# Expert outputs scattered with addition onto the residual in DRAM

## The reference

```python
h = x' + attention(layernorm(x'))                 # x' is layer 1's normalised input
z = layernorm(h); probs = softmax(z @ router)     # 4096 x 8
top_p, top_i = top_k(probs, 2); top_p /= sum(top_p)
# the rows of each expert, in order, up to cap = 1280; what is beyond is dropped
exp_in = the rows z of expert e, padded with zero rows      # 8 x 1280 x 128
exp_out = gelu(exp_in @ moe_w1[e]) @ moe_w2[e]              # 128 -> 512 -> 128
moe = zeros.at[token].add(exp_out * top_p)        # each token: at most two addends
return h + moe                                    # added to x with the other part
```

## Time and profile before

| | us |
|---|---|
| median of 3 runs | 1261.8 (1260.59 to 1263.59) |
| the profiled execution, as timed | 1267.76 |
| its span, first to last instruction | 1266.0 |
| PE busy | 986.8 (78%) |
| DVE busy | 737.2 (58%) |
| ACT busy | 625.4 (49%) |
| POOL busy | 572.5 (45%) |

### The profile page before, as it was taken

One profiled execution on the slowest core, in us unless ns is written; L12 is line 12 of the kernel. 1 busy time (PEld: TensorE's weight loads), 2 busy tenths in 40 slices (PEclk: granted clock), 3 DMA queues, 4 the chain that ended last, 5 costly groups with the idle time before them and its releaser, 6 DMA issues.

```text
span 1266.0 us, 21239 instructions
## 1 busy us (share of the span) xinstructions
PE 986.8 (78%) x6531; PEld 626.0 (49%) x6564; DVE 737.2 (58%) x1565; ACT 625.4 (49%) x1155; POOL 572.5 (45%) x633
## 2 busy tenths in 40 slices
PE   7699999873999898898989858466567785799960
PEld 4355544572444444454445335344345453699950
DVE  6677760122666566656666454897864556644435
ACT  6555554301776576666766636233256454234410
POOL 3200000268474554646632203987422757865650
PEclk9899999996999899999999979677688878799985
DMA  4011102351101011001010089000010101122216
GB/s 124 34 67 66 66 39 66 100 194 26 26 18 26 14 23 24 20 18 26 18 26 18 1 118 207 1 1 1 1 33 16 49 27 58 46 86 94 79 47 178
DMA packets 67228, 65.89 MB, mean 52 GB/s; under 512 B 6562, under 2 KB 60268, under 8 KB 65104
## 3 DMA queue, kind: packets, MB, share of 16 engines
q1 hardware_dynamic: 52560, 53.46, 15.8%
q0 software_dynamic: 4608, 6.61, 1.6%
q10 hardware_dynamic: 9984, 4.80, 1.4%
HBM read 29.90 MB, written 29.43 MB: 47 GB/s over the span
## 4 chain that ended last, share of the span: by engine, by line
PE 37%; DVE 21%; ACT 6%; issue 5%; DMA 2%; POOL 2%; DVEq 0%; SPq 0%; ACTq 0%; POOLq 0%
DVE B_mneg L1058 6%; PE banks L2069 5%; PE banks L1866 5%; PE banks L2061 4%; PE banks L1838 4%; PE banks L1887 3%; PE banks L1852 3%; PE banks L1991 3%; ACT B_qt L1511 2%; DVE D_dmx L1161 2%; DVE D_pr L1171 2%; PE banks L1944 1%; DVE D_gun L1203 1%; DMA F_back<-y_dram 1%; PE banks L1840 1%
## 5 line engine op out<-in xcount | busy, mean ns | idle before, releaser
L1058 DVE TENSOR_REDUCE B_mneg<-banks 128x2 f32<-128x256 f32 (+3 forms) x256 | 208.3, 823 | 144.6 <-PE banks L1840 138.3
L1520 ACT ACTIVATE B_pt<-banks 128x1024 f32<-128x1024 f32 (+3 forms) x256 | 177.4, 707 | 96.8 <-PE banks L1852 92.8
L724 POOL TENSOR_SCALAR_AFFINE_SELECT B_pt<-B_pt 128x512 f32<-128x512 f32 x128 | 81.4, 636 | 201.3 <-ACT B_pt L1520 195.2
L1838 PE MATMUL banks<-B_kp,B_qt 128*128 128x128 bf16 (+1 forms) x511 | 128.9, 307 | 2.1 <-DVE B_mneg L1058 0.7
L1852 PE MATMUL banks<-B_qt,B_kp 128*128 128x256 bf16 (+3 forms) x480 | 106.4, 299 | 19.0 <-DVE B_mneg L1058 14.6
L1840 PE MATMUL banks<-B_mask_q,B_identb 128*128 128x128 bf16 x512 | 103.9, 223 | 0.1
L1590 ACT ACTIVATE D_pr<-banks,D_dmx 128x512 f32<-128x512 f32 x64 | 44.0, 687 | 120.7 <-DVE D_dmx L1161 120.6
L900 POOL DMA_INDIRECT y_dram<-F_yo,F_ide x80 | 81.1, 1013 | 48.8 <-DVE F_yo L1367 24.6
L1866 PE MATMUL banks<-B_pt,B_vp 128*32 128x512 f32 (+3 forms) x1024 | 97.4, 453 | 6.0 <-issue 5.3
L858 POOL DMA_INDIRECT rows_dram<-F_xs,F_rowi x64 | 63.7, 995 | 77.2 <-DVE F_xs L1239 44.6
L694 POOL CAST B_identb<-ident 128x128 bf16<-128x128 f32 x1 | 0.3, 291 | 202.4 <-ACT C_eo L1493 202.4
(11 more groups left out here) (269 smaller groups left out, 2239.0 us busy)
## 6 DMA issues: line engine op xcount, KB each, us to landing
comb_dram<-C_comb SPq DMA_DIRECT2D x8, 1024.0 KB, 3.8
C_cst<-comb_dram SPq DMA_DIRECT2D x8, 1024.0 KB, 4.8
B_kp<-B_kt SPq DMA_DIRECT2D x64, 128.0 KB, 2.4
rows_dram<-D_zeros SPq DMA_DIRECT2D x8, 645.0 KB, 18.4
F_xe<-rows_dram SPq DMA_DIRECT2D x8, 645.0 KB, 4.0
C_w<-w_in SPq DMA_DIRECT2D x16, 256.0 KB, 2.8
y_dram<-D_zeros SPq DMA_DIRECT2D x2, 2048.0 KB, 18.4
F_gw<-mw_in SPq DMA_DIRECT2D x16, 256.0 KB, 3.0
```

The lines of the kernel that those rows point to most:

```text
L724: g.affine_select(out=w, in_=w, compare_op=ALU.is_ge, fill=0.0, base=0, pattern=[[0, G], [1, P]], channel_multiplier=-1).then_inc(B_md, 1)
L1058: v.tensor_reduce(mneg[:, g % 2, qt, 2 * hp:2 * hp + 2], banks2[pair_of_banks(item)][:, :, 0:(qt + 1) * P], X, ALU.max, negate=True).then_ ...
L1520: a.activation(pt[:, 2 * hp:2 * hp + 2, PT_AT[kt]:PT_AT[kt] + w], banks2[pair_of_banks(item)][:, :, 0:w], ACT.Exp).then_inc(B_ex, 1)
L1838: t_.matmul(dst, qt1[:, g % 2, hp, qt * P:(qt + 1) * P], kp[:, g % NG, hp, h, 0:(qt + 1) * P], start=True, stop=False)
```

## The change

A row carries its token's share as a 130th value, and its row number now names the token's row in one array `acc_dram`, 2048 spare rows and then the 4096 tokens. Empty places carry the number of a spare row of their own, so they are written too (zeros, onto the first 1280 rows, which are cleared). `y_dram` and its clearing are gone. SP stores x, with both attention parts in it, into `acc_dram` once GpSimd's sums are done, and GpSimd waits for that before it begins with the experts. VectorE multiplies the outputs by the share as it takes them out of PSUM, for which it waits until GpSimd has copied the shares. The scatters add onto `acc_dram`. Since the same token can come from two experts, GpSimd waits after each expert until its ten scatters have landed. At the end two DMAs, on SP's and on ACT's queue, copy `acc_dram` to the output, 1 MB each. The shares are worked out four times, for 1024 tokens each, within `choose`, `place_rows` and ScalarE's list.

```diff
-RW = D + 1
+RW = D + 2
 CAP = 1280
+SPARE = 2048
...
         yield t0 + 11.0, ("r", h, 0)
-    yield 216.0, ("d", 0, 0)
+        yield t0 + 10.9, ("d", h, 0)
...
@@ sync
             for e in range(EXP):
                 sp.dma_start(rows_dram[e * CAP:(e + 1) * CAP, :].rearrange("(p n) d -> p n d", p=P),
-                             zeros[:].unsqueeze(1).broadcast_to([P, CAP // P, RW])).then_inc(D_z, 16)
-
-            for k in range(2):
-                sp.dma_start(y_dram[k * B * T:(k + 1) * B * T, :].rearrange("(p n) d -> p n d", p=P),
-                             zeros[:, 0:D].unsqueeze(1).broadcast_to([P, TILES, D])).then_inc(D_z, 16)
+                             zeros[:]).then_inc(D_z, 16)
+            sp.dma_start(acc_dram[0:CAP, :].rearrange("(p n) d -> p n d", p=P),
+                         zeros[:, :, 0:D]).then_inc(D_z, 16)
...
             for par in range(2):
                 load_rows(0, par)
             sp.sem_inc(G_zf, 2)
+            sp.wait_ge(F_xo, 1)
+            for b in range(B):
+                sp.dma_start(acc_dram[SPARE + b * T:SPARE + (b + 1) * T, :].rearrange("(i p) d -> p i d", p=P),
+                             x[:, b * NT:(b + 1) * NT, :]).then_inc(G_acc, 16)
...
-            with sp.Fori(0, B) as b:
-                sp.wait_ge(G_xr, b + 1)
-                sp.dma_start(out[bass.ds(b * T, T), :].rearrange("(i p) d -> p i d", p=P),
-                             x[:, bass.ds(b * NT, NT), :]).then_inc(s_out, 16)
-            sp.wait_ge(s_out, 16 * B)
+            half = B * T // 2
+            sp.wait_ge(G_zs[0], 16 * CT * (EXP // 2))
+            sp.wait_ge(G_zs[1], 16 * CT * (EXP // 2))
+            sp.dma_start(out[0:half, :].rearrange("(p n) d -> p (n d)", p=P),
+                         acc_dram[SPARE:SPARE + half, :].rearrange("(p n) d -> p (n d)", p=P)).then_inc(s_out, 16)
+            sp.wait_ge(s_out, 16 * 2)
...
@@ gpsimd
+            pool.wait_ge(G_acc, 16 * B)
             with pool.Fori(0, EXP // 2) as pr:
                 for par in range(2):
                     pool.wait_ge(G_x[par], pr * 16 + 16)
                     pool.wait_ge(G_zf, at(pr, par, 1, 1))
                     pool.sem_inc(turns, 1)
+                    g.tensor_copy(she[:, par, :], xe[:, par, :, D + 1])
                     g.tensor_copy(ide[:, par, :], xe[:, par, :, D].bitcast(I32)).then_inc(G_id, 1)
...
-                                out=y_dram[:, :], out_offset=bass.IndirectOffsetOnAxis(ap=ide[:, par, m:m + 1], axis=0),
-                                in_=yo[:, par, m, :], in_offset=None, bounds_check=2 * B * T - 1, oob_is_err=False
-                            ).then_inc(G_zs[par], 16)
+                                out=acc_dram[:, :], out_offset=bass.IndirectOffsetOnAxis(ap=ide[:, par, m:m + 1], axis=0),
+                                in_=yo[:, par, m, :], in_offset=None, bounds_check=SPARE + B * T - 1, oob_is_err=True,
+                                compute_op=ALU.add).then_inc(G_zs[par], 16)
+                    pool.wait_ge(G_zs[par], pr * (16 * CT) + 16 * CT)
+                    pool.sem_inc(turns, 1)
...
@@ vector, choose and place_rows
                 dve.sem_inc(F_mk, 1)
+                v.tensor_tensor(e2[:, tiles], top2[:, tiles], top1[:, tiles], ALU.subtract).then_inc(F_d, 1)
...
                     own.link(v.tensor_reduce(row[:, k, tiles], one_hot[:, h], X, ALU.add))
+                shares = [xs[:, 2 * hq:2 * hq + 2, k, :, D + 1] for k in range(2)]
+                dve.wait_ge(F_e, hq + 1)
+                own.link(v.tensor_scalar(e2p[:, tiles], e2[:, tiles], 1.0, None, ALU.add))
+                own.link(v.reciprocal(shares[0], e2p[:, tiles].rearrange("p (q t) -> p q t", t=NT)))
+                v.tensor_tensor(shares[1], e2[:, tiles].rearrange("p (q t) -> p q t", t=NT), shares[0], ALU.mult)
                 for k in range(2):
...
@@ vector, the experts
                             dve.wait_ge(G_zf, it * 2 + (e + 1))
-                        v.tensor_copy(yo[:, e, n0:n0 + n, :], bank[4 + (3 * e + c) % 2][:, 0:n * D].rearrange(
-                            "p (n d) -> p n d", d=D)).then_inc(G_ys, 1)
+                            dve.wait_ge(G_id, it * 2 + (e + 1))
+                        v.tensor_tensor(yo[:, e, n0:n0 + n, :], bank[4 + (3 * e + c) % 2][:, 0:n * D].rearrange(
+                            "p (n d) -> p n d", d=D), she[:, e, n0:n0 + n].unsqueeze(2).broadcast_to([P, n, D]),
+                            ALU.mult).then_inc(G_ys, 1)
...
@@ scalar, behind the experts
-            for par in range(2):
-                act.wait_ge(G_zs[par], 16 * CT * (EXP // 2))
-            act.sem_inc(G_bu, 2)
-            with act.Fori(0, B // 2) as hb:
-                for par in range(2):
-
-                    act.wait_ge(G_bu, at(hb, par, 1, 1))
-                    for k in range(2):
-                        act.dma_start(back[:, par, k, :, :], y_dram[bass.ds(hb * (2 * T) + (par * T + k * B * T), T), :]
-                                      .rearrange("(t p) d -> p t d", p=P)).then_inc(G_bk[par], 16)
+            half = B * T // 2
+            act.wait_ge(G_zs[0], 16 * CT * (EXP // 2))
+            act.wait_ge(G_zs[1], 16 * CT * (EXP // 2))
+            act.dma_start(out[half:2 * half, :].rearrange("(p n) d -> p (n d)", p=P),
+                          acc_dram[SPARE + half:SPARE + 2 * half, :].rearrange("(p n) d -> p (n d)", p=P)
+                          ).then_inc(s_out, 16)
```

More of the change, by code:

```diff
@@ L453, in build @@
         drs, oms = Dm("drs", [P, TILES]), Dm("oms", [P, TILES])
-        zeros, junk = Dm("zeros", [P, RW]), Dm("junk", [P, 2, NT, D])
+        zeros, junk = Dm("zeros", [P, CAP // P, RW]), Dm("junk", [P, 2, NT, D])
         nmr = Dm("nmr", [P, TILES])
         desc, first_row = Dm("desc", [P, EXP]), Dm("first_row", [P, EXP])
-        ids = Dm("ids", [P, 2, TILES], I32)
+        ids = Dm("ids", [P, TILES], I32)
         tri, ones = Dm("tri", [P, P]), Dm("ones", [P, P])
         top1, top2 = Dm("top1", [P, TILES]), Dm("top2", [P, TILES])
-        share, e2 = Dm("share", [P, 2, TILES]), Dm("e2", [P, TILES])
+        e2, e2p = Dm("e2", [P, TILES]), Dm("e2p", [P, TILES])
         row = Dm("row", [P, 2, TILES])
-        kept = Dm("kept", [P, 2, TILES])
         memD1 = ctx.enter_context(ExitStack())
@@ L528, in build @@
         G_zs = [sem("G_y_scattered_even"), sem("G_y_scattered_odd")]
-        back = Fm("back", [P, 2, 2, NT, D])
-        G_bk, G_bu = [sem("G_back_even"), sem("G_back_odd")], sem("G_back_used")
-        G_xr = sem("G_x_ready")
+        G_acc = sem("G_sums_begun")
         memF.close()
@@ L796, in _ @@
             own.link(g.memset(zeros[:], 0.0))
-            g.iota(zeros[:, D:RW].bitcast(I32), pattern=[[0, 1]], base=2 * B * T, channel_multiplier=0).then_inc(D_z, 1)
+            g.iota(zeros[:, :, D].bitcast(I32), pattern=[[1, CAP // P]], base=0, channel_multiplier=CAP // P).then_inc(D_z, 1)
             own.link(g.memset(sc[:], NEG))
@@ L854, in scatter_rows @@
                 if q == 0:
-                    pool.wait_ge(D_z, 16 * (EXP + 2) + 1)
+                    pool.wait_ge(D_z, 16 * (EXP + 1) + 1)
                 for t in range(NT):
@@ L1235, in deviations @@
                                        op1=ALU.mult).then_inc(F_r, 1)
-                dve.wait_ge(F_const, 5)
+                dve.wait_ge(F_const, 4)
             def row_ids(q):
-                v.tensor_copy(xs[:, q, :, :, D].bitcast(I32), ids[:, :, q * NT:(q + 1) * NT]).then_inc(F_id, 1)
+                v.tensor_copy(xs[:, q, :, :, D].bitcast(I32), ids[:, q * NT:(q + 1) * NT].unsqueeze(1)
+                              .broadcast_to([P, 2, NT])).then_inc(F_id, 1)
             def wide(small):
@@ L1285, in place_rows @@
                 ins.then_inc(F_row, 1)
-            def shares():
-                v.tensor_tensor(e2[:], top2[:], top1[:], ALU.subtract).then_inc(F_d, 1)
-                own.link(v.tensor_scalar(kept[:], row[:], float(EXP * CAP), None, ALU.is_lt))
-                dve.wait_ge(F_e, 1)
-                own.link(v.tensor_scalar(share[:, 0], e2[:], 1.0, None, ALU.add))
-                own.link(v.reciprocal(share[:, 0], share[:, 0]))
-                own.link(v.tensor_tensor(share[:, 1], e2[:], share[:, 0], ALU.mult))
-                own.link(v.tensor_tensor(share[:], share[:], kept[:], ALU.mult))
             for kind, a_, n in D_PLAN.order:
@@ L1326, in _ @@
                     place_rows(a_)
-                elif kind == "d":
-                    shares()
             dve.wait_ge(D_rms, 1)
@@ L1375, in _ @@
             own.end_loop(EXP // 2)
-            dve.wait_ge(F_xo, 1)
-            with dve.Fori(0, B // 2) as hb:
-                own.loop(hb, 2 * 2)
-                for par in range(2):
-                    dve.wait_ge(G_bk[par], hb * 32 + 32)
-                    for k in range(2):
-                        for t in range(NT):
-                            i = hb * (2 * NT) + (par * NT + t)
-                            xi = x[:, bass.ds(i, 1), :].squeeze(1)
```

(11 more changed lines are left out.)

7 lines of the change are left out of this document (3 added, 4 removed).

## The result

The changed kernel takes 1298.85 us (median of 4 runs, 1298.53 to 1299.29), the kernel before on the same chip 1262.69 us (4 runs, 1260.59 to 1264.27): ratio 1.0288, interval 1.0270 to 1.0305. So it is slower by 36 us, where 1254.0 was forecast, and it lies above the end of the range, 1286. The profiled execution of after took 1299.29 us as timed, its span is 1297.5 us; before has 1266.0. The medians lie further apart (36 us) than the spans (31.5 us), since the profiled execution of the kernel before was 5 us longer than its median (1267.76 and 1262.69).

The account below looks back on a forecast made before the run. TensorE was taken to bound the experts at 16.92 us each, GpSimd close behind. Last landing 1240.5 + 8v plus a 9.7 us tail gave 1258.2 us span with v = 1.0, median 1254.0; range 1244 to 1286 us.

Parts of the forecast that it names:

- v: Extra cost of ten adding scatters over ten plain ones, up to their landing: taken as 1.0 us, ends 0 and 6.9.
- term 1: Clearing at 739 us: the larger zero tile costs nothing, covered by GpSimd's idle time; 1.1 us without that cover.
- term 2: Shares worked out with the rows: 0.7 us more on the chain from the last row numbers to GpSimd's sums.
- term 3: Start of the experts: GpSimd waits 9.0 us for the stored x, bounds 6.9 and 16.6 us.
- R: Time when expert 0's row numbers and shares are copied and ready: 1108.1 us.
- term 4: Experts' loop: GpSimd's round closes on itself through landing, copies and eviction, 16.62 us plus v, against TensorE's 16.92 us.
- term 5: End of the kernel: two DRAM to DRAM copies replace the 35.5 us tail, leaving 9.7 us.
- The sum: Whole span: 1250.2 + 8v, so 1258.2 us with v = 1.0, 7.8 us below 1266.0.
- The frame: Step from profiled span to median: median taken 4.2 us below the span, differences carried over one to one.
- the adding scatter takes longer to issue: Rival, in each expert's ten GpSimd scatters: slower from v = 2.0, median 1274 us at a quarter more; chance 0.34.
- The half rate: Skill rule for the scatters' transfers: adding runs at half a copy's rate, 0.14 us more per scatter, span 1252 us.
- many descriptors can be emitted before the cost shows: Skill rule on the scatters' issue on GpSimd: many descriptors before extra cost shows; the trace of before cannot confirm it.

Follow-up runs that it names:

- wide sums: Changed kernel with plain scatters into y_dram, no waits between experts, 16 fetches issued at once, 512-column additions at the end: 1250.45 us, ratio 0.9904.
- copies and start ahead: Changed kernel, each expert's copies before the previous landing, expert 0's before GpSimd's last sum, wait for x at first scatter: 1287.1 us, ratio 1.0201.

## Why the prediction was wrong

The sign was wrong, and one term did it: the size of v.

- **Clearing (term 1), nothing: right.** The larger memset took 1.18 us, and GpSimd still stood 3.19 us for the weights two instructions behind it. The transfers got shorter for a second reason, which the prediction didn't name: `rows_dram` used to be cleared in pieces of 516 bytes, at 136 to 145 GB/s (745 to 775 us), and is now cleared in pieces of 5200 bytes, at 379 to 412 GB/s (740 to 755 us).
- **Shares (term 2), +0.7 us: not tested.** VectorE's three operations in the last choice take 0.17, 0.21 and 0.17 us. GpSimd's sums began 3.4 us earlier than before in this execution (1064.26, 1067.62); over the kernels on chips without stops that event lies between 1059.9 and 1069.0, so 0.7 us can't be seen in it.
- **Store of x (term 3), 9.0 us: right.** GpSimd stood 9.19 us. The start R was 1103.9, not 1108.1, most of it the earlier routing. TensorE stopped 7.14 us where I said about 6, behind VectorE's eviction, as described.
- **The round (term 4) closes on GpSimd: right in its form.** In the changed kernel all eight first evictions waited for GpSimd's copies, and the landing stands in the chain of waits in every round. The 16.6 us with plain scatters are near the 16.62 forecast for v = 0, but they don't prove it: TensorE had no gap there and needs 16.92 us itself (the copies, late at first, catch up with it).
- **v: the step that failed.** "The nearest row is the scatter of the same shape, so I take no more for the issue." Taken was v = 1.0, all of it landing. Measured is 23.20 - 16.62 = 6.6 us. The landing part was 0.5 (3.33 us from issue to landing, less 2.25 before, less 0.57 of longer issue). The issue part, taken as nothing with 4.9 as its upper end, is 5.8: ten times 0.57 to 0.60. What is left, some 0.3, wasn't followed up. The row showed a plain scatter's price, and I carried it to an operation of which no row showed anything. Half as much again was too low an end as well: it is 57 to 59% (1590 and 1615 against 1013 ns).
- **The tail (term 5), 9.7 us: right.** 9.0 us, at 351 GB/s read and written together.
- **The sum.** The formula was span = 1250.2 + 8v. With v = 6.6 it gives 1303.0; less 4.2 us for the earlier R and 0.7 for the tail, 1298. The span is 1297.5. So the accounting of the span holds, and v alone turned the sign. The 3.4 us of earlier routing are luck that no term foresaw: without them the miss would be 3.4 us larger.
- **The frame, 4.2 us from span to median: too much.** The median is 1.35 us above the span of after, and not 4.2 below it, since the profiled execution of before was a long one of its kind. That is 5.5 of the 44.9 us between 1254.0 and 1298.85; v is behind the rest.

The rival "the adding scatter takes longer to issue" is what happened, at its place and by its mechanism, with "half more" at 1293 us. It had 0.34, and the forecast 0.41 with a value for the issue at the low end of its own bounds. The range, too, stopped at v = 5.0 (1286 us), though the ends given for v reach 6.9, which makes 1301 us on the median: the measured 6.6 lies inside these ends and outside the range. With each 0.1 us of the issue worth 8 us of span, an operation that no row showed deserved the middle of those bounds: v = 3.5 gives 1278 us for the span, and the other sign.

The half rate: an adding scatter takes more of the DMA engines, and more than by a factor of two. Queue 0 was busy for 5.4% of 16 engines' 1297.5 us, 1121 us; with plain scatters in the same kernel 2.1% of 16 x 1244.1, 418 us. The difference, 703 us over 80, is 8.8 us of engine time on top of a plain scatter's 2.9 (418 / 144, those of the routing taken in): four times as much, 0.73 us per engine and scatter. In the kernel before, with the addition alone (3.8% against 1.6%), it is three and a half times. That is still hidden under 1.85 us between scatters. The rule in the Trainium skill, Collectives: The Full Stack, part 3 (a reduce at half a copy's rate), points the right way and is too mild here: 0.14 us more per engine and scatter by the prediction's working from it, 0.55 measured (8.8 / 16).

The Trainium skill's rule in DMA: Bandwidth & Descriptors (anatomy of one DMA), that many descriptors can be emitted before the cost shows, isn't contradicted by these runs: 64 rows more cost GpSimd 0.07 us in a plain scatter and 0.13 us in an adding one. It holds nothing on the fixed price of the addition, some 0.43 us, which decided here. That the packets cause this price isn't shown: with 64 rows the addition brought 48 more packets and cost 0.50 us, with 128 rows 112 more and 0.57 us. What GpSimd does in that time stays open.

## What to carry to other kernels

Before a scatter is turned into one that adds, price its issue as an operation of its own: here 1.55 us on GpSimd in place of 0.98, with an extra for the addition that is nearly the same for 64 rows as for 128, so it pays only where the issuing engine has that time to spare per instruction. A wait for a landing was free while its engine had slack (ratio 1.0004), and with the engine as the bound the new waits cost 3.3 us per round; two changes that are cheap one by one can be dear together (9.4 and 28.0 us, but 61.4). And the gain of a change like this may lie in a part that can stand alone: the shares multiplied in on the way out of PSUM and two wide sums behind the last landing kept 11 of the 26 us, with no addition in the DMA.

## What the runs showed that was not expected

Three chips take 1320 to 1335 us for the kernel before. Up to about 900 us the kernels run there as elsewhere; then ScalarE, TensorE and VectorE stand for 4 to 12 us at a time, in the routing and in the experts. ScalarE's activation in the experts on such a chip, between 900 and 1290 us (wide sums, then the changed kernel):

```profile
L1656 ACT ACTIVATE F_gh<-banks 128x512 f32<-128x512 f32 (+1 forms) x96 | 47.6, 528 | 121.3 <-PE banks L2050 73.5 <-remote 47.2
```

```profile
L1651 ACT ACTIVATE F_gh<-banks 128x512 f32<-128x512 f32 (+1 forms) x96 | 50.0, 526 | 118.0 <-PE banks L2046 113.8
```

47.2 us are idle time that ends with nothing the trace shows on this core. The wide sums have such time on the chip of the changed kernel's row too (33.3 us in this group); in the changed kernel none is put down to it. A reading that fits, but isn't shown: its engines already wait for GpSimd there, and the stops fall into those waits. The table fits it as well: the changed kernel loses 2.9% on an ordinary chip and 0.4% there, and the version with copies and start ahead loses 2.0% on an ordinary chip and gains 0.7 to 2.0% on the others. The cause of the stops stays open. Of the versions that compute all of the reference, wide sums alone gained on every chip that it ran on.
